# Block scales of the feed-forward weights prepared on GpSimd instead of VectorE in a perceiver layer

## The reference, cut to what matters

```python
def fake_quant_nvfp4(x, global_scale):
    xb = x.reshape(sh[:-1] + (sh[-1] // 16, 16))
    amax = jnp.max(jnp.abs(xb), axis=-1, keepdims=True)
    sc = jnp.clip(amax / 6.0 * global_scale, 0.0, 448.0)
    sc8 = sc.astype(jnp.float8_e4m3fn).astype(jnp.float32)
    dq = sc8 / global_scale
    safe_dq = jnp.where(dq == 0.0, 1.0, dq)
    a = jnp.clip(jnp.abs(xb) / safe_dq, 0.0, 6.0)
    q = jnp.sign(xb) * _FP4_VALS[jnp.digitize(a, _FP4_MIDS)]
    return (q * dq).reshape(sh)
def nvfp4_linear(x, w, s_in):
    s_w = 448.0 * 6.0 / jnp.max(jnp.abs(w))
    return jnp.einsum('bsh,oh->bso', fake_quant_nvfp4(x, s_in), fake_quant_nvfp4(w, s_w))

x = x + xattn(layernorm(x), ctx_1024, ...)   # the long loop over the context
x = x + attn(layernorm(x), ...)              # cumsum of k * v, gated
x = x + ffn(layernorm(x), ...)               # silu(gate) * up, then down: three nvfp4_linear
```

## Time and profile before

| | us |
|---|---|
| median of 3 runs | 488.05 |
| lowest and highest run | 487.03, 488.24 |
| span of the profiled execution | 485.6 |
| median less that span: what lies around it | 2.45 |
| VectorE busy | 446.5 (92%) |
| TensorE busy | 383.7 (79%) |
| ScalarE busy | 361.3 (74%) |
| GpSimd busy | 8.1 (2%) |

### The profile page before, as it was taken

The page is one execution under the profiler, slowest core; times in us unless marked ns, Lnnn a source line. Parts: engine busy times, 40 slices in busy tenths (PEclk is TensorE's granted clock), DMA queues, the critical chain, the costliest instruction groups (busy, mean ns, idle before and its releaser), DMA issues.

```text
span 485.6 us, 5951 instructions
## 1 busy us (share of the span) xinstructions
PE 383.7 (79%) x1877; PEld 303.2 (62%) x1880; DVE 446.5 (92%) x686; ACT 361.3 (74%) x950; POOL 8.1 (2%) x25
## 2 busy tenths in 40 slices
PE   0796757998997997997997997991999789637754
PEld 0585546886885886885886885891986445313333
DVE  4559999999999999999999999999998869899993
ACT  1359887998998988988978888885437577666764
POOL 2100100000000000000000000000000000000000
PEclk9999887999999999999999999996799999868888
DMA  7930500040140040040041041022020000000001
GB/s 234 355 103 1 173 0 2 24 129 23 34 135 7 22 130 22 12 137 26 5 132 39 2 130 45 1 90 85 0 88 0 0 3 0 1 0 0 24 22 43
DMA packets 27070, 27.65 MB, mean 57 GB/s; under 512 B 1184, under 2 KB 26784, under 8 KB 27040
## 3 DMA queue, kind: packets, MB, share of 16 engines
q1 hardware_dynamic: 26736, 27.27, 17.7%
q0 software_dynamic: 160, 0.01, 0.0%
q10 hardware_dynamic: 144, 0.00, 0.0%
HBM read 26.22 MB, written 1.05 MB: 56 GB/s over the span
## 4 chain that ended last, share of the span: by engine, by line
DVE 75%; issue 11%; PE 8%; ACT 5%; POOL 1%; POOLq 0%
DVE focus_words L1247 8%; DVE focus_words L1263 8%; DVE sorted L1286 4%; DVE level L1272 4%; DVE level L1273 4%; DVE merge L1299 4%; DVE sorted L1287 4%; DVE sorted L1191 3%; DVE amax L1160 2%; DVE sorted L1292 2%; DVE sorted L1291 2%; DVE keymax L1289 2%; DVE merge L1297 2%; PE bank L808 2%; DVE rank L1310 2%
## 5 line engine op out<-in xcount | busy, mean ns | idle before, releaser
L808 PE MATMUL bank<-WkT,rows_T 128*128 128x256 f32 x512 | 127.1, 396 | 32.9 <-ACT rows_T L426 32.9
L808 PEld LDWEIGHTS bank<-WkT,rows_T 128*128 128x128 f32 x512 | 96.8, 197 | 50.4 <-ACT rows_T L426 38.5
L902 PE MATMUL bank<-ctx_words,focus_words 128*128 128x257 f32 x512 | 115.6, 384 | 3.5 <-ACT focus_words L525 3.5
L902 PEld LDWEIGHTS bank<-ctx_words,focus_words 128*128 128x128 f32 x512 | 99.7, 197 | 16.2 <-ACT focus_words L525 5.5
L513 ACT ACTIVATE focus_words<-focus_words,shift,ff 128x256 f32<-128x256 f32 x136 | 79.8, 590 | 0.6
L479 ACT ACTIVATE focus_words<-bank 128x256 f32<-128x256 f32 x136 | 50.2, 381 | 27.3 <-PE bank L808 27.3
L525 ACT ACTIVATE focus_words<-focus_words,row_scale 128x256 f32<-128x256 f32 x136 | 56.2, 513 | 12.8 <-DVE row_scale L1265 12.8
L426 ACT ACTIVATE rows_T<-bank 128x512 f32<-128x512 f32 x78 | 44.4, 595 | 18.4 <-PE bank L781 18.4
L1247 DVE SCALAR_TENSOR_TENSOR focus_words<-focus_words,key_and,key_xor 128x2048 int32<-128x2048 int32 x17 | 39.9, 2345 | 8.2 <-ACT focus_words L479 8.2
L781 PE MATMUL bank<-ident,ctx_words 128*128 128x128 f32 x256 | 38.4, 279 | 3.8 <-DMA ctx_words<-in_ctx_dram 3.1
L1330 DVE TENSOR_TENSOR mask<-focus_words,fifth 128x2048 bf16<-128x2048 f32 x17 | 39.0, 2292 | 0.5
(11 more groups left out here) (192 smaller groups left out, 586.3 us busy)
## 6 DMA issues: line engine op xcount, KB each, us to landing
ctx_words<-in_ctx_dram SPq DMA_DIRECT2D x32, 512.0 KB, 3.9
ctx_words<-in_L_ffn_gate_w_dram SPq DMA_DIRECT2D x2, 1024.0 KB, 7.9
ctx_words<-in_L_ffn_up_w_dram SPq DMA_DIRECT2D x2, 1024.0 KB, 8.8
xs<-in_x_dram SPq DMA_DIRECT2D x4, 256.0 KB, 5.0
ctx_words<-in_L_ffn_down_w_dram SPq DMA_DIRECT2D x2, 512.0 KB, 9.5
ctx_words<-in_L_ffn_down_w_dram SPq DMA_DIRECT2D x1, 1024.0 KB, 5.0
out_dram<-xs SPq DMA_DIRECT2D x3, 256.0 KB, 2.1
gateT<-in_L_attn_W_qkv_dram SPq DMA_DIRECT2D x1, 512.0 KB, 6.3
```

The source lines that it names most:

```text
L808: ins = pe.matmul(proj_bank[m][:, t * D:(t + 1) * D], rows_T[:, m % 2, 2 * t + k, :], WT[:, k, :], start=(k == 0), stop=(k == KT - 1))
L902: ins = pe.matmul(sum_bank[k][:, 0:GW], heads_half(expo[slot][:, t, :], k), ctx_ring[:, s, t, :], start=(s == 0 and t == 0), stop=(s == PE ...
```

## The change

VectorE loses `weight_scales()` between `mix(1)` and `mix(2)`, and the first two of the three instructions of `weight_reciprocals()`. Four small instructions remain of them (`tensor_scales`: three reciprocals of 2 or 3 columns and one multiplication), and they move into the loop, ahead of `compare_pairs(3)`. GpSimd waits for the last of them and then issues 15 instructions of its own: seven of 1 to 3 columns, one of 128 columns (`ident_out`), and seven of 384 columns, of which four are `tensor_tensor` (two tensor inputs) and three `tensor_scalar` (one). A semaphore `pstep` orders them, so each of the wide ones waits until the one before it has finished. `out_undo` is now a product instead of a reciprocal. ScalarE's `spread_fp8` waits on a semaphore of its own for the weights; VectorE's `weight_reciprocals` waits on `w_undone` and keeps the large reciprocal.

```diff
@@ block.gpsimd, after partition_all_reduce
             pool.wait_ge(small_loaded, 64)
+            pool.wait_ge(w_scale_ready, 1)
+            pool.tensor_scalar(in_sixth[:, :], in_scale[:, :], 1.0 / FP4_MAX, None, ALU.mult).then_inc(pstep, 1)
+            pool.tensor_scalar(in_undo[:, :], in_scale_inv[:, :], NEARLY_ONE / HALF_WAY, None, ALU.mult).then_inc(pstep, 1)
+            pool.tensor_scalar(w_sixth[:, :], w_scale[:, :], 1.0 / FP4_MAX, None, ALU.mult).then_inc(pstep, 1)
+            pool.tensor_scalar(w_undo[:, :], w_scale_inv[:, :], NEARLY_ONE / HALF_WAY, None, ALU.mult).then_inc(pstep, 1)
...
+            pool.tensor_scalar(out_undo[:, :], w_scale[:, 2:3], in_scale[:, 1:2], 1.0 / UNITS_LEFT,
+                               ALU.mult, ALU.mult).then_inc(pstep, 1)
+            pool.wait_ge(pstep, 7)
+            pool.tensor_scalar(ident_out[:, :], ident[:, :], out_undo[:, 0:1], None, ALU.mult).then_inc(ident_out_ready, 1)
+            pool.tensor_tensor(w_amax[:, :, :], w_amax[:, :, :], each(w_sixth), ALU.mult).then_inc(pstep, 1)
+            pool.wait_ge(pstep, 8)
+            pool.tensor_scalar(w_amax[:, :, :], w_amax[:, :, :], FP8_MAX, None, ALU.min).then_inc(pstep, 1)
+            pool.wait_ge(pstep, 9)
+            pool.tensor_scalar(flat_w(w_magic), flat_w(w_amax), FP8_MAGIC, FP8_LEAST, ALU.mult, ALU.max).then_inc(pstep, 1)
+            pool.wait_ge(pstep, 10)
+            pool.tensor_tensor(flat_w(w_amax), flat_w(w_amax), flat_w(w_magic), ALU.add).then_inc(pstep, 1)
+            pool.wait_ge(pstep, 11)
+            pool.tensor_tensor(flat_w(w_fp8), flat_w(w_amax), flat_w(w_magic), ALU.subtract).then_inc(w_fp8_ready, 1)
+            pool.wait_ge(w_fp8_ready, 1)
+            pool.tensor_tensor(w_rcp[:, :, :], w_fp8[:, :, :], each(w_undo), ALU.mult).then_inc(pstep, 1)
+            pool.wait_ge(pstep, 12)
+            pool.tensor_scalar(w_rcp[:, :, :], w_rcp[:, :, :], TINY / HALF_WAY, None, ALU.max).then_inc(w_undone, 1)
@@ block.scalar, spread_fp8
-                act.wait_ge(fp8_rounded, max(i - 1, 1))
+                if i < 3:
+                    act.wait_ge(w_fp8_ready, 1)
+                else:
+                    act.wait_ge(fp8_rounded, i - 2)
@@ block.vector
+            def tensor_scales():
+
+                dve.wait_ge(small_loaded, 64)
+                dve.wait_ge(absmax_reduced, 1)
+                step(dve.reciprocal(in_scale_inv[:, :], in_scale[:, :]))
+                then(dve.reciprocal(w_scale[:, :], w_absmax_all[:, :]))
+                then(dve.tensor_scalar(w_scale[:, :], w_scale[:, :], FP8_MAX * FP4_MAX, None, ALU.mult))
+                dve.reciprocal(w_scale_inv[:, :], w_scale[:, :]).then_inc(w_scale_ready, 1)
+
             def pair(a, last):
...
+                if a == 3:
+                    tensor_scales()
                 compare_pairs(a)
...
-            def weight_scales():
...
             def weight_reciprocals():
 
-                settle()
-                then(dve.tensor_tensor(w_rcp[:, :, :], w_fp8[:, :, :], each(w_undo), ALU.mult))
-                then(dve.tensor_scalar(w_rcp[:, :, :], w_rcp[:, :, :], TINY / HALF_WAY, None, ALU.max))
+                dve.wait_ge(w_undone, 1)
                 then(dve.reciprocal(w_rcp[:, :, :], w_rcp[:, :, :]))
...
             mix(0)
             mix(1)
-            weight_scales()
             mix(2)
```

More of the change, by code:

```diff
@@ L218, in perceiver_layer @@
         w_max_taken = sem("w_max_taken")
+        w_scale_ready = sem("w_scale_ready")
+        pstep = sem("pstep")
+        w_fp8_ready = sem("w_fp8_ready")
+        w_undone = sem("w_undone")
         front_loaded = [sem(f"front_loaded{s}") for s in range(PER_BATCH)]
@@ L280, in perceiver_layer @@
         EVERY, LOWER, UPPER = slice(0, T), slice(0, T // 2), slice(T // 2, T)
+        each = lambda a: a[:, :].rearrange("p (w o) -> p w o", o=1).broadcast_to([P, 3, P])
+        flat_w = lambda a: a[:, :, :].rearrange("p w b -> p (w b)")
         NORM_TILES = (EVERY, LOWER, UPPER, LOWER, UPPER)
@@ L408, in _ @@
             pool.wait_ge(small_loaded, 64)
+            pool.wait_ge(w_scale_ready, 1)
[3 more added lines that the diff above has]
+            pool.tensor_scalar(w_undo[:, :], w_scale_inv[:, :], NEARLY_ONE / HALF_WAY, None, ALU.mult).then_inc(pstep, 1)
+            pool.tensor_scalar(out_scale[:, 0:2], w_scale_inv[:, 0:2], in_scale_inv[:, 0:1], UNITS_LEFT,
+                               ALU.mult, ALU.mult).then_inc(pstep, 1)
+            pool.tensor_scalar(out_scale[:, 2:3], w_scale_inv[:, 2:3], in_scale_inv[:, 1:2], UNITS_LEFT,
+                               ALU.mult, ALU.mult).then_inc(pstep, 1)
+            pool.tensor_scalar(out_undo[:, :], w_scale[:, 2:3], in_scale[:, 1:2], 1.0 / UNITS_LEFT,
+                               ALU.mult, ALU.mult).then_inc(pstep, 1)
+            pool.wait_ge(pstep, 7)
[13 more added lines that the diff above has]
+            pool.tensor_scalar(w_rcp[:, :, :], w_rcp[:, :, :], TINY / HALF_WAY, None, ALU.max).then_inc(w_undone, 1)
             pool.wait_ge(quad_in_sbuf, group_quad(ATT_BEHIND[1] + 1, 0))
@@ L1449, in add_batch @@
                 attention_stats(m)
-            each = lambda a: a[:, :].rearrange("p (w o) -> p w o", o=1).broadcast_to([P, 3, P])
-            flat_w = lambda a: a[:, :, :].rearrange("p w b -> p (w b)")
-            def weight_scales():
[L1456 to L1476, removed]
             def weight_reciprocals():
-                settle()
-                then(dve.tensor_tensor(w_rcp[:, :, :], w_fp8[:, :, :], each(w_undo), ALU.mult))
-                then(dve.tensor_scalar(w_rcp[:, :, :], w_rcp[:, :, :], TINY / HALF_WAY, None, ALU.max))
+                dve.wait_ge(w_undone, 1)
                 then(dve.reciprocal(w_rcp[:, :, :], w_rcp[:, :, :]))
```

## The result

The changed kernel takes 483.45 us (median of 4 runs, 482.30 to 483.92), the kernel before 487.68 us beside it (487.03 to 488.24). The ratio is 0.9907, with a 95% interval of 0.9891 to 0.9924: faster by 0.9%. The forecast was 492.4 us, 487.1 to 496.2, so the time lies outside the range, on the other side of no change.

The account below looks back on a forecast made before the run. It took VectorE to bound the loop and TensorE's chain the tail. Span 485.6 + 0.53 (loop) - 0.48 (tail) + 4.25 (GpSimd contention) = 489.9, plus 2.45 around it = 492.4 us; range 487.1 to 496.2.

Parts of the forecast that it names:

- What bounds the kernel now: Loop, 53 to 349 us: VectorE full, each added microsecond reaches the end; tail: the chain runs through TensorE.
- What comes to GpSimd: Fifteen GpSimd instructions after about 91 us, perhaps beginning only near 100, some 50 us long; added waits cost nothing.
- What comes to VectorE in the loop: Four small instructions between pair(1) and compare_pairs(3): +0.53 us, reaching the end in full.
- What GpSimd's work does to VectorE: In the loop, VectorE stands still while GpSimd's wide instructions run: 7 x 0.58 + 0.19 = 4.25 us, bounds 0 to 8.1.
- What goes from VectorE in the tail: 5.03 us leave VectorE's tail, but TensorE's project_out holds it until 357.04, so only 0.48 us is gained.
- The cover of GpSimd's results: Results ready near 150 us, first needed by VectorE's large reciprocal, at 362.79 before: some 200 us of cover.
- The sum: Whole kernel: 485.6 + 0.53 - 0.48 + 4.25 = 489.9 us of span, plus 2.45 around it = 492.4 us.
- The rivals: No contention, 488.1 us (0.32); tail returns all VectorE loses, 483.6 us (0.07); larger GpSimd price, over 496.2 us (0.05).
- the second: Tail: TensorE's queue ends with VectorE instead of project_out, so 4.5 us are won, 483.6 us; chance 0.07.

Follow-up runs that it names:

- experiment 1: Kernel before plus one GpSimd tensor_scalar of one column behind the reduction over the partitions, result unused: 481.23 us, ratio 0.9876.
- experiment 2: Changed kernel plus a second reduction over the partitions, result unused, at the end of GpSimd's queue: 491.38 us, ratio 1.0075 to the kernel before.
- experiment 6: experiment 1's kernel plus two memsets and 14 GpSimd tensor_scalar (one input) of 384 columns beside VectorE's loop: 484.77 us, ratio 0.9938 to before.
- experiment 7: experiment 1's kernel plus two memsets and 14 GpSimd tensor_tensor (two inputs) of 384 columns beside VectorE's loop: 491.86 us, ratio 1.0086 to before.
- experiment 3: Kernel before, weight_scales and first two instructions of weight_reciprocals moved on VectorE ahead of compare_pairs(3), GpSimd untouched: 492.40 us, ratio 1.0098.
- experiment 4: experiment 1's kernel with output scales and ident_out moved behind add_batch(2), all on VectorE: 480.39 us, ratio 0.9853.
- experiment 5: experiment 1's kernel plus two memsets and 14 further GpSimd memsets of 384 columns beside VectorE's loop: 481.64 us, ratio 0.9870 to before.

## Why the prediction was wrong, point by point

- **What bounds the kernel now**: right for the loop and the tail. But the reading began at 53 us. The stretch ahead, where VectorE's first four digits are 4, 5, 5 and 9, was never asked what it waits for. This is the step at which the forecast was lost.
- **What comes to GpSimd** is the step that had the row in its hand and took the wrong thing from it. It cited the 9.1 us of "issue" ahead of L389, saw that the changed queue has one more preparing row, and drew from both only that the new chain may begin some 9 us late, under cover. It did not follow who waits for L389 in the trace (TensorE, whose first row is released by GpSimd at 15.23), and took for granted that the wait stays as it was because the instructions around it stay. Experiments 1 and 2 show that one further instruction behind the reduction takes it away (0.50 us in place of 9.11) and that a reduction at the end of the queue brings it back (11.38 us). The missing term is 5.58 us at TensorE's start; the other 0.94 of the 6.52 belongs to the one execution. The late begin of the new chain did not come either: GpSimd's first small instruction started at 84.56, when VectorE's last one (84.19) had ended.
- **What comes to VectorE in the loop**: forecast 0.53 us, measured 0.55.
- **What GpSimd's work does to VectorE**: the mechanism was right in kind (VectorE's rows beside GpSimd's wide ones take up to 1.74 us where they took 1.22), the term 4.25 us was mis-sized; the stretched rows make 2.72. The slope of 1.51 ns per column was drawn between an `affine_select` and a memset, so between two kinds of instruction, and from GpSimd's own lengths, which are not the price. It stood for one-input instructions, which in fact cost 0.30 us for 384 columns where it gave 0.58; it also counted 0.19 for `ident_out` (128 columns), beside which no VectorE row is longer. For two inputs it was too low, 0.58 where 0.80 were measured. By the prices of experiments 6 and 7 the seven instructions would cost up to 4 x 0.80 + 3 x 0.30 = 4.1 us. The table of the loop says where the 1.4 us less come from: 0.68 at L433, in whose time `keymax` stood; 0.28 and 0.23 at the two instructions with a broadcast operand (L427 and L437); 0.08 and 0.11 at L435 and L431. `keymax` was not held in experiment 7 either; what a broadcast operand or bf16 spares by itself was not tried.
- **What goes from VectorE in the tail**: forecast -0.48, measured -0.59 for the whole tail, whose scatter of 1.3 us hides such a size, and -0.69 at `sum_group(16)`, where it is clear. The 0.21 beyond the wait of 0.48 are `mixed_quad(2)` following the products at once: it starts 0.16 us before the end that the profile gives for `project_out`, and the next starts 0.05 us sooner behind it. The next thing that is late was named rightly (`project_out`), and experiment 3 shows it apart from GpSimd.
- **The cover of GpSimd's results**: it held. The chain ended at 105.7 us, not near 150 as was worked out; the large reciprocal on VectorE came at 356.94 and waited for nothing of GpSimd's.
- **The sum**: with the missing term it would have been 492.4 - 5.6 = 486.8, and with the contention as measured 485.3; the measured medians are 483.45 and, for the kernel before, 487.68 in place of 488.05. The 1.8 us that are left can be placed. The prediction took 2.45 us for what lies around the span, from the median of three runs and the span of a single execution. Where time and span of the same run are on record, it is 1.69 to 1.79 us in the 15 runs of the kernel before that stand beside the experiments, and 1.70 to 1.80 in the four of the changed kernel: this term was some 0.7 us too large. Another 0.94 are the products with `WqT` in the profiled execution of before, and 0.11 the tail. So the profiled executions close: 485.6 - 6.52 + 3.31 - 0.59 = 481.8, and the run with that span took 483.50.
- **The rivals**: the second (483.6 us) has nearly the time, by a cause that the runs exclude. No rival named the start.

What each part of the change is worth, then: the earlier start that comes with it about -5.8 us (experiment 1), its work on GpSimd +2.7, the four small instructions +0.55, the tail -0.6. That is -3.1 us, where the medians differ by -4.2 (by the interval of the ratio -3.7 to -5.3) and the profiled executions by -3.8, of which 0.94 is not the change's. About 1 us between the parts and the medians stays open; the runs of the two kernels spread over 1.2 and 1.6 us. The part that gave the gain is not the one that the change is about, and one column of work on GpSimd gives it without the rest.

## What to carry to other kernels

Read the first microseconds like any other stretch: here an "issue" idle of 9.11 us ahead of GpSimd's first instruction that is no memset, with TensorE waiting for what GpSimd makes there, was a cost that an edit far away in GpSimd's queue took off (0.50 us, experiment 1) or brought back (11.38 us, experiment 2). If a program's GpSimd queue holds a reduction over the partitions and ordinary instructions, try one with an ordinary instruction behind the last reduction, where nobody waits for GpSimd: in experiment 1 one column of work there waited 7.69 us unseen and the kernel was 5.84 us faster. Work moved to GpSimd beside a full VectorE is not free: for 384 columns VectorE was held for 0.30 us with one tensor read and 0.80 with two, and not at all with none, while GpSimd took about 1.6 us for either of the first two. Price it by the tensors that it reads, not by how long GpSimd takes for it.

## What the runs showed of the hardware that had not been expected

Whether GpSimd waits ahead of its first `affine_select` went, in all nine kernels, by its last instruction that is neither a memset nor a DMA. Where that is a `tensor_scalar` or a `tensor_tensor` (the changed kernel, experiments 1 and 4 to 7) the wait is 0.50 us; where it is the reduction over the partitions it is 9.11, 9.51 and 11.38 us (the kernel before, experiments 3 and 2). The five kernels in which the next instruction behind the reduction is a `tensor_scalar` that waits for no other engine show 7.69 to 8.16 us ahead of it (experiments 1 and 4 to 7). The one reduction whose wait isn't hidden by another stood 5.96 us (experiment 2, at 353.58). What sets these differences stays open, and so does what GpSimd does in these waits, of which the traces show the length only.

VectorE's hold went by what GpSimd reads: 0 for writing 384 columns (experiment 5), 0.30 us for one input of 384 columns (experiment 6), 0.80 us for two (experiment 7), at one and the same VectorE instruction of 1.22 us; so the second input cost more than the first. An 8-column `tensor_scalar` of VectorE was held nearly as long as a wide instruction (0.74 us with two inputs, 0.96 where it takes 0.22); a reduction of 512 columns was not (0.67 us in experiment 7 and in the changed kernel).
